# Low-rank factors as stacked f16 parts, weight maxima spread differently over the batches, and two more PSUM banks for the queries of batch 1

## The chip, the cores and the metric

The kernel runs on one core of a Trainium2 chip. Its engines work from queues of their own and wait for each other by semaphores: TensorE (PE; matrix products into PSUM), VectorE (DVE), ScalarE (ACT), GpSimd (POOL) and SyncE (SP; it only issues transfers here). The metric is the device time of one launch in microseconds; lower is better. TensorE's clock is granted at one of two levels, 1.2 and 2.4 GHz; the profile shows it as a share of the full one.

## What is computed

Eight batches of 256 tokens and 512 channels pass two layers. The first is attention with AdaLN and a 4-bit feed-forward with low-rank additions, the second a scan (Runge-Kutta) and a mixture of experts. The change is all in the first:

```python
xn = _rms_norm(x, g_norm) * (1.0 + scale) + shift
q, k, v = heads(xn @ W_qkv)                    # 16 heads of 32
q, k = _rms_norm(q, g_q), _rms_norm(k, g_k)
o = softmax(q @ k.T * d ** -0.5) @ v
x1 = o + o @ W_out
w_up = dequant4bit(w_up_q, w_up_scale).T       # (q - 7.5) * scale, 512 x 2048
y1 = x1 @ w_up + b_up + x1 @ w_up_lora_a @ w_up_lora_b      # rank 16
x2 = relu(y1)
w_down = dequant4bit(w_down_q, w_down_scale).T # 2048 x 512
y2 = x2 @ w_down + b_down + x2 @ w_down_lora_a @ w_down_lora_b
x = x + y2
...
x = x + moe(scan(cond, cond, x), Wr, Wg, Wu, Wd, Sg, Su, Sd, Wsg)
```

## The kernel before

Channels lie on the 128 partitions, tokens along the free dimension. Layer 0 (`layer0`) handles one batch after the other; each engine has its program written out by hand, and the order in it is the order of work. A batch has a part of projections and norms (chunks c = 0 to 3 of 4 heads: q and k into one PSUM bank, their squares summed per head by `head_norm`, the root by ScalarE, the product by VectorE) and a part of heads (16, in 4 groups: scores of a group, row maxima, exponentials, transposition on TensorE, copy back, weighted sums). From batch 2 on the feed-forward of the batch two before is cut in parts and put between these. Batch 0 and batch 1 have no feed-forward beside them.

**Preparing the feed-forward's weights, in batch 0.** The low-rank products are folded into the weights: W = codes x scale + A·B. There are 16 pieces of 1024 columns (8 of the up, 8 of the down weights); four are prepared in the projections of batch 0, the others with its heads 0 to 11. A piece h passes: SP loads codes and scales into one of three staging buffers (it waits until `split` of piece h - 3 is done); VectorE `unpack` (line 735); TensorE `lora` (line 521) makes two products of 512 columns in banks D[0] and D[1], f32, 16 rows deep, once `stage` says that the correction of h - 1 has read the banks; VectorE `correct` (line 743) adds them; ScalarE `weights_high` (line 383) rounds to f16; GpSimd (line 290) subtracts for the low part. VectorE's order in a head is correct(h + 4), unpack(h + 5), copy of the transposed head, and the row maximum of the group's fourth head stands behind the first copy. The factors are scaled once, by VectorE (lines 728, 729).

**Weight maxima.** The second layer's weights (33 tiles of 3 parts, 256 KB each) are read twice. First only their largest value is taken: `part_max` (line 748) is one VectorE reduction of 128x512 per part, with four loads in flight; SP loads the next when a maximum is done. `max_parts(b, at)` gives each of batches 1, 2 and 3 a third of them, 33: four after each chunk of the projections (16), and 17 spread over the 16 heads. The second reading, from batch 4 on, splits them in f16 parts.

**Banks.** Eight PSUM banks: X[0:4], Ob[0:2], D[0:2]. Queries and keys of chunk c go to Gb[c % 2] = X[c % 2], so the projection of chunk c >= 2 waits for `d_qk` of chunk c - 2. D holds low-rank products in batch 0 and feed-forward sums from batch 2 on.

## Time and profile before

| | us |
|---|---|
| median of 3 runs | 2924.39 (2912.39 to 2925.42) |
| profiled execution | 2920.94 |
| its span, first to last instruction | 2919.2 |
| PE busy | 2779.1 (95%) |
| DVE busy | 1766.6 (61%) |
| ACT busy | 1125.0 (39%) |
| POOL busy | 1334.0 (46%) |

The span is from the first to the last instruction on any engine; the execution's time has 1.7 us more around it. "PE" is the products, "PEld" the loading of the stationary operand, which overlaps them; "SPq" is SP's issuing of transfers, "x16" a number of instructions in a row that the view merges. In a timeline row the brackets tell how long the engine was idle before, and what it waited for. Names left of the arrow are written, names right of it read; `l0bank` are the eight PSUM banks, `carry` the workspace, `w_emb` also holds the normed queries and keys, `hid` and `parts_mem` are staging, `late` is where the factors lie. Batch 0's projections begin at 25.7 us, its heads at 63; batch 1 at 168, its heads at 202; batch 2 at 256.

### The profile page before, as it was taken

How to read it: one execution, taken by the hardware profiler on the slowest of the kernel's cores; microseconds unless marked ns; L12 is line 12 of the kernel's file. 1: busy time of each engine (PE TensorE's matmuls, PEld its weight loads, DVE VectorE, ACT ScalarE, POOL GpSimd, SP SyncE). 2: the span in 40 equal slices, each digit the busy share in tenths (PEclk: the TensorE clock that was granted, in tenths of full speed). 3: DMA queues.
4: the chain of work that ended last, by engine and by line, in shares of the span. 5: the costliest groups of instructions: out<-in, count | busy, mean ns of one | idle time of the engine just before them, and what ended most of it. 6: DMA issues, size and time to landing. Idle time of an engine off the chain costs nothing.

```text
span 2919.2 us, 131794 instructions
## 1 busy us (share of the span) xinstructions
PE 2779.1 (95%) x49488; PEld 2428.8 (83%) x49488; DVE 1766.6 (61%) x6291; ACT 1125.0 (39%) x4986; POOL 1334.0 (46%) x3467
## 2 busy tenths in 40 slices
PE   8877999998989999999999999999999999999998
PEld 5345776776777778999999999999999999999987
DVE  3645664565464556666666666666666666666654
ACT  2323344465444433334334333333433433433322
POOL 2310001111114666665666666666666666666600
PEclk8579999999999998999999999999999999999999
DMA  7422234354340003444443443443444444344376
GB/s 241 145 87 86 82 102 135 107 168 132 124 130 4 3 4 98 131 128 134 129 129 127 134 132 120 143 130 126 135 127 132 134 128 129 127 134 129 122 234 201
DMA packets 137226, 360.85 MB, mean 124 GB/s; under 512 B 15888, under 2 KB 24720, under 8 KB 136592
## 3 DMA queue, kind: packets, MB, share of 16 engines
q1 hardware_dynamic: 136336, 354.17, 38.5%
q8 instruction: 149, 2.44, 0.3%
q10 hardware_dynamic: 672, 3.67, 0.3%
q14 instruction: 69, 0.57, 0.1%
HBM read 323.31 MB, written 34.47 MB: 123 GB/s over the span
## 4 chain that ended last, share of the span: by engine, by line
PE 59%; POOL 5%; issue 3%; DVE 2%; ACT 0%; DMA 0%; POOLq 0%; DVEq 0%; SPq 0%
PE pscan L1360 12%; PE pd L1313 12%; PE pg L1265 12%; PE pscan L1356 11%; PE pu L1265 11%; POOL lin L1110 1%; POOL lin L1126 0%; POOL carry L1155 0%; POOL from_q L1122 0%; POOL lin L1120 0%; POOL lin L1132 0%; POOL from_q L1128 0%; POOL from_q L1137 0%; PE prouter L1375 0%; POOL lin L1141 0%
## 5 line engine op out<-in xcount | busy, mean ns | idle before, releaser
L1356 PEld LDWEIGHTS pscan<-th,carry 128*128 128x128 f16 x16384 | 550.9, 96 | 73.0 <-ACT th L1175 52.6
L1356 PE MATMUL pscan<-th,carry 128*128 128x8 f16 x16384 | 560.2, 166 | 20.4 <-ACT th L1175 9.7
L1360 PE MATMUL pscan<-th,carry 128*128 128x16 f16 x16384 | 558.2, 169 | 1.9 <-DVE th L1471 1.1
L1360 PEld LDWEIGHTS pscan<-th,carry 128*128 128x128 f16 x16384 | 482.2, 96 | 3.2 <-DVE th L1471 3.0
L1175 ACT ACTIVATE th<-state 128x32 f16<-128x32 f32 x768 | 176.0, 229 | 689.7 <-DVE state L1488 689.6
L1313 PE MATMUL pd<-hg,wbuf 128*128 128x256 f16 x3168 | 427.8, 274 | 2.3 <-DMA wbuf<-w_split 2.3
L1265 PE MATMUL pg<-qh,wbuf 128*128 128x256 f16 x3168 | 424.6, 273 | 0.0
L1265 PE MATMUL pu<-qh,wbuf 128*128 128x256 f16 x3168 | 423.1, 272 | 0.0
L1488 DVE TENSOR_REDUCE state<-pscan 128x32 f32<-128x96 f32 x768 | 197.5, 257 | 264.8 <-PE pscan L1360 261.2
L1265 PEld LDWEIGHTS pg<-qh,wbuf 128*128 128x128 f16 x3168 | 293.6, 97 | 34.9
L1265 PEld LDWEIGHTS pu<-qh,wbuf 128*128 128x128 f16 x3168 | 292.3, 97 | 31.9
L1313 PEld LDWEIGHTS pd<-hg,wbuf 128*128 128x128 f16 x3168 | 277.6, 98 | 31.5 <-issue 2.6
L1483 DVE SCALAR_TENSOR_TENSOR pscan<-pscan,lin 128x32 f32<-128x32 f32 x1024 | 203.9, 199 | 109.8 <-DVE pscan L1474 3.4
L1471 DVE TENSOR_TENSOR th<-pact,th 128x32 f16<-128x32 f32 x1024 | 190.7, 186 | 125.9 <-ACT pact L1176 122.8
L1143 POOL TENSOR_TENSOR from_q<-state,carry 128x32 f32<-128x32 f32 x256 | 90.9, 355 | 263.0 <-DVE state L1488 263.0
L1175 ACT ACTIVATE th<-carry 128x32 f16<-128x32 f32 x256 | 58.6, 229 | 333.2 <-DVE carry L1488 323.4
L444 ACT ACTIVATE w_emb<-l0bank,nmax 128x256 f32<-128x256 f32 x256 | 118.7, 475 | 134.5 <-DVE nmax L816 134.5
L296 POOL TENSOR_SCALAR spare<-parts_mem 128x512 f16<-128x512 f16 x33 | 50.8, 1538 | 258.8 <-DMA w_split<-spare 151.4
L1526 DVE SCALAR_TENSOR_TENSOR hp<-hb,wk,gates 128x256 f32<-128x256 f32 x264 | 158.0, 599 | 17.7 <-DVE hb L1519 7.6
L1137 POOL TENSOR_TENSOR from_q<-state,carry 128x64 f32<-128x64 f32 x256 | 86.3, 337 | 167.4 <-DVE state L1488 167.4
L1240 ACT ACTIVATE hg<-hp 128x256 f16<-128x256 f32 x264 | 109.7, 416 | 136.7 <-DVE hp L1526 136.7
L314 POOL PARTITION_ALL_REDUCE fs<-fs x8 | 3.0, 378 | 324.3 <-DVE fs L861 324.3
(232 smaller groups left out, 4937.1 us busy)
## 6 DMA issues: line engine op xcount, KB each, us to landing
wbuf<-w_split SPq DMA_DIRECT2D x264, 512.0 KB, 3.5
wbuf<-w_split SPq DMA_DIRECT2D x264, 384.0 KB, 3.1
parts_mem<-in_w_tiles SPq DMA_DIRECT2D x149, 256.0 KB, 3.1
w_split<-parts_mem SPq DMA_DIRECT2D x99, 256.0 KB, 2.8
late<-in_w_tiles SPq DMA_DIRECT2D x49, 256.0 KB, 3.1
w_split<-spare SPq DMA_DIRECT2D x33, 128.0 KB, 3.0
out<-oo SPq DMA_DIRECT2D x8, 512.0 KB, 3.6
xs<-in_x SPq DMA_DIRECT2D x1, 3584.0 KB, 14.4
```

The costliest lines, as they stand in the source:

```text
L444: ins = act.activation(pr[:, h % HPC, qc, :], X[h % HPC][:, qc * T:(qc + 1) * T], ACT.Exp, bias=nmax[:, h % HPC, qc:qc + 1], accum_out=psu ...
L1143: pl.tensor_tensor(ms4[:], state[3][:], c4[:], ALU.mult).then_inc(S["pchain"], 1)
L1175: act.activation(th[:, :, 0, :], v3(src[:]), ACT.Tanh, scale=unit).then_inc(S["th_ready"], 1)
L1240: act.activation(hg[:, slot, 0, :], hp[:], ACT.Identity, scale=2.0 ** -11).then_inc(S["hi_ready"], 1)
L1265: ins = mm(dst[:, 0:GT], wgu[:, slot, a, w, k, :], qh[:, q, k, :], start=(k == 0 and w == q), stop=(k == NC - 1 and w == 1))
L1313: ins = mm(pd[m // 2][:, (m % 2) * GT:(m % 2 + 1) * GT], wd[:, slot, w, m * P:(m + 1) * P], hg[:, slot, h, :], start=False, stop=False, sk ...
L1356: mm(pscan[:, 0, m * B:(m + 1) * B], clo[:, k, m * P:(m + 1) * P], th[:, k, 0, :], start=(m == 0 and k == 0), stop=False, skip_group_check ...
L1360: ins = mm(pscan[:, 0:2, m * B:(m + 1) * B], chi[:, k, m * P:(m + 1) * P], th[:, k], start=False, stop=(k == NC - 1), skip_group_check=True)
L1471: dve.tensor_tensor(th[:, :, 1, :], v3(t32), th[:, :, 0, :], ALU.subtract).then_inc(S["tl_ready"], 1)
L1483: chain(dve.scalar_tensor_tensor(pscan[:, 2, 0:W], cub, -RK[s - 1] / 3, A[u][:, s, :], ALU.mult, ALU.add), False)
L1488: dve.tensor_reduce(nxt[:], pscan[:, 0:3, 0:W].rearrange("p a w -> p w a"), AX.X, ALU.add).then_inc(S["q_ready"], 1)
L1526: dve.scalar_tensor_tensor(hp[:], hb[:], wk[:, 4:5], g, ALU.mult, ALU.mult).then_inc(S["hp_ready"], 1)
```

## The change

**Factors.** The host stacks each pair of factors three times over 80 rows, with rows of zeros between: rows 0 to 15, 32 to 47, 64 to 79. ScalarE makes an f16 rounding of all 80 rows of A and of B (`factors_high`), each with a scale that is a power of two; VectorE then replaces rows 64 to 79 of A and rows 32 to 47 of B by the f16 remainders (`low_of`). One f16 product 80 rows deep so sums high·high + high·low + low·high. Up factors are made before the first product, down factors inside the projections of batch 0. The stacks are loaded into a part of `w_dn` that isn't in use yet.

**Maxima.** `max_parts` gives batch 1 the first 16 (four per chunk, none in the heads), batch 2 the next 42, batch 3 the last 41.

**Banks.** In batch 1 alone, chunks 2 and 3 of q and k go to D[0] and D[1] (`gbank`).

```diff
-        lora_up, lora_dn = late[0:R, 0:N + H0], late[32:32 + R, 0:N + H0]
+        stacked = [w_dn[0:5 * R].rearrange("p a h n -> p (a h n)").bitcast(F32)[:, n * (N + H0):(n + 1) * (N + H0)] for n in range(2)]
+        factors = [late[0:5 * R, n * (N + H0) // 2:(n + 1) * (N + H0) // 2].bitcast(F16) for n in range(2)]
+        fa = [factors[0][:, 0:N], factors[1][:, 0:H0]]
+        fb = [factors[0][:, N:N + H0], factors[1][:, H0:H0 + N]]
...
+        def gbank(b, c):
+            return (Gb + D)[c] if isinstance(b, int) and b == 1 else Gb[c % 2]
...
         def max_parts(b, at):
-            return spread((b - 1) * TILES, TILES, at, 4, PARTS) if 1 <= b <= 3 else []
+            first, count = {1: (0, 16), 2: (16, 42), 3: (58, 41)}.get(b, (0, 0))
+            return spread(first, count, at, 4, PARTS) if count else []
...
-            for half, factors in enumerate((lora_up, lora_dn)):
-                sp.dma_start(factors, dram["lora"][half]).then_inc(S["lora"], 16)
+            sp.dma_start(stacked[0], dram["lora"][0]).then_inc(S["lora0"], 16)
             for h in range(PIECES):
                 u = h % 3
+                if h == 2:
+                    sp.dma_start(stacked[1], dram["lora"][1]).then_inc(S["lora1"], 16)
...
+            def factors_high(n):
+                act.wait_ge(S["lora_scale"], 1)
+                act.wait_ge(S["lora0"] if n == 0 else S["lora1"], 16)
+                cut = N if n == 0 else H0
+                act.activation(fa[n], stacked[n][:, 0:cut], ACT.Identity, scale=for_a[0:5 * R, n:n + 1])
+                act.activation(fb[n], stacked[n][:, cut:], ACT.Identity, scale=for_b[0:5 * R, n:n + 1]).then_inc(S["lora_high"], 1)
...
+                    if b == 1 and c >= 2:
+                        act.wait_ge(S["d_qk"], b * NC + c - 1)
                     act.activation(rh[:, c % 2], Rb[c % 2][:].rearrange("p (a t) -> p a t", a=2), ACT.Ln, scale=1.0 / DH, bias=eps).then_inc(S["achain"], 1)
...
+                    if not b and c == 1:
+                        factors_high(1)
...
             norm(0)
+            factors_high(0)
...
             def lora(h):
-                if h == 0:
-                    pe.wait_ge(S["lora_ok"], 1)
-                else:
+                if h % (PIECES // 2) == 0:
+                    pe.wait_ge(S["lora_ok"], h // (PIECES // 2) + 1)
+                if h:
                     pe.wait_ge(S["stage"], h)
...
-                        c, col = h // 2, N + h % 2 * PIECE + i * 512
-                        a, bb = lora_up[:, c * P:(c + 1) * P], lora_up[:, col:col + 512]
+                        c, col = h // 2, h % 2 * PIECE + i * 512
+                        a, bb = fa[0][:, c * P:(c + 1) * P], fb[0][:, col:col + 512]
...
-                    if c >= 2:
+                    if c >= 2 and gbank(b, c) is Gb[c % 2]:
                         pe.wait_ge(S["d_qk"], b * NC + c - 1)
...
+                link(dve.tensor_scalar(power, pairs[:, :, 1], 2.0 ** -60, None, ALU.max))
+                link(dve.tensor_scalar(kp2[:, 128:130], kp2[:, 128:130], 0x7F800000, None, ALU.bitwise_and))
+                link(dve.reciprocal(for_b, power))
+                link(dve.tensor_scalar(for_b, for_b, 0.25, None, ALU.mult))
+                link(dve.scalar_tensor_tensor(for_a, power, 4.0, fs[:, 15:17], ALU.mult, ALU.mult))
+                dve.sem_inc(S["lora_scale"], 1)
...
-                dve.wait_ge(S["lora"], 32)
-                dve.tensor_scalar(lora_up[:, 0:N], lora_up[:, 0:N], swu[0:R, :], None, ALU.mult)
-                dve.tensor_scalar(lora_dn[:, 0:H0], lora_dn[:, 0:H0], swd[32:32 + R, :], None, ALU.mult).then_inc(S["lora_ok"], 1)
+                low_of(0)
+
+            def low_of(n):
+                dve.wait_ge(S["lora_high"], n + 1)
+                cut = N if n == 0 else H0
+                a, bb = fa[n][4 * R:5 * R], fb[n][2 * R:3 * R]
+                dve.scalar_tensor_tensor(a, stacked[n][4 * R:5 * R, 0:cut], for_a[4 * R:5 * R, n:n + 1], a, ALU.mult, ALU.subtract)
+                dve.scalar_tensor_tensor(bb, stacked[n][2 * R:3 * R, cut:], for_b[2 * R:3 * R, n:n + 1], bb, ALU.mult, ALU.subtract).then_inc(S["lora_ok"], 1)
...
                         correct(c)
+                        if c == 2:
+                            low_of(1)
```

VectorE's queue at the opening, from the last scaling of biases to the first correction, before (L728 and L729 scale the factors, L735 unpacks, L743 corrects):

```order
L726 TENSOR_SCALAR vecs<-vecs,fs 128x16
L728 TENSOR_SCALAR late<-late,fs 16x512
L729 TENSOR_SCALAR late<-late,fs 16x2048
L735 SCALAR_TENSOR_TENSOR hid<-hid 128x1024
L743 SCALAR_TENSOR_TENSOR hid<-hid,fs,l0bank 128x512 x2
```

and in the changed kernel (L760 and L761 are the low parts, L767 unpacks, L775 corrects):

```order
L753 TENSOR_SCALAR vecs<-vecs,fs 128x16
L760 SCALAR_TENSOR_TENSOR late<-w_dn,spare,late 16x512
L761 SCALAR_TENSOR_TENSOR late<-w_dn,spare,late 16x2048
L767 SCALAR_TENSOR_TENSOR hid<-hid 128x1024
L775 SCALAR_TENSOR_TENSOR hid<-hid,fs,l0bank 128x512 x2
```

Two scalings in place became two subtractions, behind ScalarE's roundings; the down factors' pair stands behind the third correction now. The order of products on TensorE is the same.

VectorE's queue in the first group of heads of batch 1, before (L816 is a row maximum, L829 the copy, L748 a weight maximum, L819 the inverse of the sums):

```order
L816 TENSOR_REDUCE nmax<-l0bank 128x2 x3
L829 COPY carry<-l0bank 128x512
L748 TENSOR_REDUCE spare<-parts_mem 128x1
L816 TENSOR_REDUCE nmax<-l0bank 128x2
L829 COPY carry<-l0bank 128x512
L748 TENSOR_REDUCE spare<-parts_mem 128x1
L829 COPY carry<-l0bank 128x512
L748 TENSOR_REDUCE spare<-parts_mem 128x1
L819 RECIPROCAL rinv<-psum_e 128x8
L829 COPY carry<-l0bank 128x512
L748 TENSOR_REDUCE spare<-late 128x1
```

and in the changed kernel (L850, L863 and L853 for L816, L829 and L819):

```order
L850 TENSOR_REDUCE nmax<-l0bank 128x2 x3
L863 COPY carry<-l0bank 128x512
L850 TENSOR_REDUCE nmax<-l0bank 128x2
L863 COPY carry<-l0bank 128x512 x2
L853 RECIPROCAL rinv<-psum_e 128x8
L863 COPY carry<-l0bank 128x512
```

The four weight maxima of a group are gone; those of the projections stay as they were.

The same engine and group in batch 2, in the changed kernel (L780 is the weight maximum, L806 the hidden's low part):

```order
L863 COPY carry<-l0bank 128x512
L780 TENSOR_REDUCE spare<-parts_mem 128x1
L806 TENSOR_TENSOR hid<-l0bank,hid 128x2x256
L850 TENSOR_REDUCE nmax<-l0bank 128x2
L863 COPY carry<-l0bank 128x512
L780 TENSOR_REDUCE spare<-parts_mem 128x1 x2
L806 TENSOR_TENSOR hid<-l0bank,hid 128x2x256
L863 COPY carry<-l0bank 128x512
L780 TENSOR_REDUCE spare<-late 128x1
L853 RECIPROCAL rinv<-psum_e 128x8
L863 COPY carry<-l0bank 128x512
L780 TENSOR_REDUCE spare<-parts_mem 128x1 x2
```

Before, one maximum stood where there are two now.

## Rows read from the trace of the kernel before

**Rows 1.** Windows of the opening: length; busy PE, PEld, DVE, ACT, POOL; clock; DMA; GB/s.

```profile
63.00:89.00 26.00, 18.17 (x49) 7.50 (x48) 16.54 (x22) 8.86 (x22) 9.43 (x5) 0.59 0.93 288
89.00:116.00 27.00, 22.65 (x88) 11.08 (x88) 15.93 (x23) 9.74 (x24) 8.83 (x5) 0.63 0.48 147
116.00:142.00 26.00, 24.02 (x80) 10.09 (x80) 14.01 (x22) 7.72 (x22) 7.94 (x4) 0.50 0.30 92
168.00:202.00 34.00, 25.00 (x92) 16.37 (x95) 14.52 (x29) 9.77 (x15) 4.03 (x5) 0.98 0.24 78
202.00:245.00 43.00, 26.13 (x232) 16.72 (x232) 34.80 (x64) 18.19 (x70) 0.00 (x0) 0.78 0.41 120
256.00:344.00 88.00, 81.99 (x693) 64.31 (x695) 56.54 (x102) 38.31 (x109) 4.03 (x5) 1.00 0.31 93
```

**Rows 2.** Groups of instructions by line and shape, first 330 us: busy, mean ns, idle before.

```profile
L521 PE MATMUL l0bank<-late 16*128 16x512 f32 x64 | 47.8, 884 | 8.0 <-DVE parts_mem L743 4.9 <-DVE hid L743 3.1
L535 PE MATMUL l0bank<-late,w_up 128*128 128x256 f16 x192 | 23.3, 273 | 0.8 <-DVE hid L774 0.8
```

**Rows 3.** Timeline, one step of batch 0: start, length, engine, line, operation, idle before.

```profile
102.83 1.22 DVE L735 SCALAR_TENSOR_TENSOR hid<-hid 128x1024 f32<-128x1024 int32 x1
102.95 1.06 ACT L383 ACTIVATE w_dn<-hid 128x1024 f16<-128x1024 f32 x1 [1.58 <-DVE hid L743]
104.08 2.12 POOL L290 TENSOR_TENSOR w_dn<-hid,w_dn 128x1024 f16<-128x1024 f32 x1 [2.82 <-ACT w_dn L383]
109.06 3.78 PE L521 MATMUL l0bank<-late 16*128 16x512 f32 x4 [0.91 <-DVE hid L743]
112.88 1.40 DVE L743 SCALAR_TENSOR_TENSOR parts_mem<-parts_mem,fs,l0bank 128x512 f32<-128x512 f32 x2 [2.03 <-PE l0bank L521]
```

**Rows 4.** One timeline row of SP's queue; sizes and time to landing of two transfers.

```profile
106.61 2.38 SPq L226 DMA_DIRECT2D hid<-in_dn_s  x4
...
hid<-in_dn_s SPq DMA_DIRECT2D x20, 128.0 KB, 3.6
xs<-in_x SPq DMA_DIRECT2D x1, 3584.0 KB, 14.4
```

**Rows 5.** Timeline of the first group of heads of batch 0, VectorE and GpSimd.

```profile
72.26 1.22 DVE L735 SCALAR_TENSOR_TENSOR parts_mem<-parts_mem 128x1024 f32<-128x1024 int32 x1 [4.64 <-DMA parts_mem<-in_up_s]
82.44 2.12 POOL L290 TENSOR_TENSOR w_up<-hid,w_up 128x1024 f16<-128x1024 f32 x1 [2.49 <-ACT w_up L383]
82.84 2.80 DVE L735 SCALAR_TENSOR_TENSOR hid<-hid 128x1024 f32<-128x1024 int32 x1 [1.56 <-DMA hid<-in_up_s]
```

**Rows 6.** Timeline of the opening, VectorE and TensorE.

```profile
28.61 1.28 DVE L729 TENSOR_SCALAR late<-late,fs 16x2048 f32<-16x2048 f32 x1
31.54 1.98 PE L521 MATMUL l0bank<-late 16*128 16x512 f32 x4
40.31 5.41 PE L574 MATMUL l0bank<-carry,w_qkv 128*128 128x256 f32 x16 [0.38 <-DVE w_emb L808]
```

**Rows 7.** Timeline of batch 1, projections and first scores.

```profile
184.92 3.72 PE L574 MATMUL l0bank<-carry,w_qkv 128*128 128x256 f32 x16 [2.29 <-DVE w_emb L808]
201.75 2.09 PE L601 MATMUL l0bank<-w_emb 32*128 32x256 f32 x16 [4.43 <-DVE w_emb L808]
204.27 0.69 DVE L748 TENSOR_REDUCE spare<-parts_mem 128x1 f32<-128x512 f32 x1 [1.08 <-DMA parts_mem<-in_w_tiles]
```

**Rows 8.** Timeline of batch 1, the third group of heads ends.

```profile
231.26 0.68 DVE L748 TENSOR_REDUCE spare<-parts_mem 128x1 f32<-128x512 f32 x1
231.86 0.68 DVE L829 COPY carry<-l0bank 128x512 f32<-128x512 f32 x1
233.85 1.15 PE L601 MATMUL l0bank<-w_emb 32*128 32x256 f32 x16 [1.33 <-DVE carry L829]
```

**Rows 9.** Timeline of batch 2, heads, one wait of TensorE.

```profile
312.09 1.49 PE L535 MATMUL l0bank<-late,w_up 128*128 128x256 f16 x12 [0.23 <-DVE hid L774]
```

More of the change, by code:

```diff
@@ L142, in layer0 @@
         largest = spare[:, 0:3 * TILES]
+        power, for_a, for_b = spare[:, 128:130], spare[:, 130:132], spare[:, 132:134]
         bank = [ctx.enter_context(nc.psum_tensor(f"l0bank{i}", [P, 512], F32)) for i in range(8)]
@@ L155, in layer0 @@
                  "chain achain seq plseq "
-                 "mm_lora scaled stage split d_bounds g_bounds lora_ok "
+                 "mm_lora scaled stage split d_bounds g_bounds lora_scale lora_high lora_ok "
                  "part_in0 part_in1 part_in2 part_in3 part_out0 part_out1 part_out2 part_hi part_done part_third third_out widest gmax wscale state_in mx par coef setup").split()
@@ L416, in square @@
                     act.wait_ge(S["p_qk"], b * NC + c + 1)
-                    act.activation(sqh[:, c % 2], Gb[c % 2][:].rearrange("p (a t) -> p a t", a=2), ACT.Square).then_inc(S["a_sq"], 1)
+                    act.activation(sqh[:, c % 2], gbank(b, c)[:].rearrange("p (a t) -> p a t", a=2), ACT.Square).then_inc(S["a_sq"], 1)
                 def values():
@@ L1627, in arranged @@
     part = lambda a: np.moveaxis(rows(a), 0, 1)
+    gap = np.zeros((R, N + H0), np.float32)
+    stack = lambda m: np.concatenate([m, gap, m, gap, m], 0)
     up_q, dn_q = g("L0_ffn_w_up_q").T, g("L0_ffn_w_down_q").T
@@ L1632, in arranged @@
         "up_q": part(up_q), "dn_q": part(dn_q), "up_s": g("L0_ffn_w_up_scale").T, "dn_s": g("L0_ffn_w_down_scale").T,
-        "lora": np.stack([np.concatenate([g("L0_ffn_w_up_lora_a").T, g("L0_ffn_w_up_lora_b")], 1),
-                          np.concatenate([g("L0_ffn_w_down_lora_a").T, g("L0_ffn_w_down_lora_b")], 1)]),
+        "lora": np.stack([stack(np.concatenate([g("L0_ffn_w_up_lora_a").T, g("L0_ffn_w_up_lora_b")], 1)),
+                          stack(np.concatenate([g("L0_ffn_w_down_lora_a").T, g("L0_ffn_w_down_lora_b")], 1))]),
         "vecs": np.concatenate([part(g("cond_2048").T).reshape(P, NC * B), part(g("L0_cond_b_emb")), part(g("L0_cond_g_norm")),
```

11 lines of the change are left out of this document (6 added, 5 removed).

## The prediction

> **What bounds the kernel now.** I read the page first: TensorE is busy for 95% of the span, and most of the chain that ended last is TensorE in the second layer, which the change doesn't touch. Everything that it touches lies in the first 344 us, so the next view was a table of windows over that stretch [rows 1]. The reader is to see two regimes. From 256 us on (batch 2, the first with feed-forward products beside the attention) TensorE is busy 82 of 88 us at the full 2.4 GHz: that stage is bound by it. In batch 0 (here 63 to 142 us) and in the heads of batch 1 (202 to 245) it is not: it is busy 26 of 43 us in the latter, while VectorE is busy 35 of 43; in batch 0 the granted clock is 0.50 to 0.63, the lower level of 1.2 GHz for most of the time. A stage with no engine full is bound by hand-overs, so the third view was the timeline of a single step.
>
> A step of batch 0's heads [rows 3] is a ring between two engines. The two low-rank products of a piece (L521) start at 109.06 and take 3.78 us; VectorE's correction L743, which reads them, starts at 112.88 and takes 1.40; the next piece's product may start only then, since both use banks D. That makes 5.3 us a step, four steps are 21 us, and the other 5.2 us of a group of four heads are its scores and the weighted sums of the group before. Two groups (89 to 116, 116 to 142) take 27 and 26 us [rows 1]. The first group, 63 to 89, looks alike and isn't: its transfers are busy 0.93 of the time at 288 GB/s, and VectorE waits 4.64 us for the codes of a piece [rows 5], which queue behind the load of all other batches' x, 3584 KB that take 14.4 us to land [rows 4].
>
> **The low-rank product, heads of batch 0.** A piece has 2 products of 512 columns. As f32 they leave four records in the trace, 64 in all for 16 pieces, busy 47.8 us, 2.99 a piece. An f16 product of 256 columns is busy 23.3/192 = 0.121 us [rows 2], so 512 columns take 0.24; two take 0.49 us, or 0.97 at the lower clock, where this stage runs. 80 rows instead of 16 cost nothing, as I take it, since those f16 rows use 128. TensorE is rid of 32 to 40 us; that is the far end of the gain, not the gain.
>
> With the ring's step at 0.97 + 1.40 + 0.1 = 2.5 us, VectorE is next: per head a correction 1.40, an unpacking 1.22 [rows 3] and a copy 0.69, 3.1 us from start to start since neighbours overlap by nearly 0.1, and one more row maximum (0.6) per group. A group becomes 5.2 + 4 x 3.1 + 0.6 + 0.6 (hand-overs) = 18.8 us, if nothing else is late.
>
> Something is. Staging has three buffers, so the unpacking of piece h+3 needs the correction of h to have gone on through ScalarE (1.06), GpSimd (2.12), SP's issue (0.33 and 2.38 for five transfers) and the landing (3.6 from its own issue, so 0.6 before SP's end counts) [rows 3, 4]: 1.06 + 2.12 + 0.33 + 2.38 - 0.6 + 3.6 + 0.3 for three hand-overs = 9.2 us. VectorE comes to it after two steps, 6.2 to 6.7 us, within a group: a wait of about 2.8 us once per group (across a group's border the 5.2 us cover it). I add 0.5 for VectorE and GpSimd in each other's way: an unpacking that started 0.4 us into a GpSimd subtraction took 2.80 us, not 1.22, and ended 1.1 us after it [rows 5]. So a group takes 22.1 us and two groups 44.2, against 53: **8.8 us gained**. The ends: 0, if the loop of loads is longer than I think, and 15 us (two groups at 18.8).
>
> The Trainium skill has that last effect as a rule (GPSIMD Engine Reference, "Specifications": GpSimd's SBUF interfaces are shared with VectorE and contend with instructions that have two SBUF inputs). It speaks against this change, since shorter steps put more unpackings beside subtractions, and the two new low parts have two SBUF inputs too. Were every unpacking of the two groups held as that one was, 1.6 us, it would make 8 x 1.6 = 12.8 us and eat the whole gain of this term; the trace has one such case in 16.
>
> The group at 63 to 89 I take at 0 (ends -3 and +2): the order of bytes behind x stays, and its VectorE waits for them.
>
> **The opening.** SP now loads 800 KB of stacked factors ahead of piece 0 (before 2 x 160 KB) and as much again before piece 2. ScalarE makes the high parts (80x512 and 80x2048: 0.6 and, from 1.06 for 1024 columns, 2.0 us), VectorE adds five scalar steps (0.2 each) ahead and two low parts behind (0.7 and, from the 1.22 us of 1024 columns, 2.3) where it had two scalings, of which the larger took 1.28 [rows 6]. So the first product starts at about 33.7 instead of 31.54, but is 1.5 us shorter; behind it in TensorE's queue stand the second projection and all of batch 0, which come about 1 us late. The second projection's queries gate the third, which waited 0.38 us for VectorE [rows 6] and will wait more, so shorter products gain nothing there. The same work for the down factors lies behind the third correction, where VectorE waits for a head norm anyway. Later products give back 2 us before the scores at 63, and the wait for x's bytes swallows the difference: **0** (-2 to +4, the latter if TensorE's gap of 2 us leaves the next projection at the lower clock, where the same 16 records took 5.41 us and not 3.72 [rows 6, 7]).
>
> **Batch 1, projections.** Queries of chunks 2 and 3 go to D, so the two waits of 2.29 us before them go [rows 7]: 4.6 us. Late next: the norms through ScalarE and, between VectorE's multiplications, four maxima each, which are still there, and whose loads (four deep) land in about the time in which they are used. Before, the last four waited 1.08 us for theirs and held the first row maximum; they start earlier now, while the scores' 2.09 us run. **5.7 us gained** (ends 3 and 7).
>
> **Batch 1, heads.** VectorE loses 17 maxima. A maximum takes 0.68 us and puts the next copy 0.60 later [rows 8]. Four per group stood there; the one behind the fourth copy lay under the scores. Three are on the path to the fourth copy, after which TensorE had waited 1.33 us [rows 8]: at most 1.8 us a group. Without them the fourth head's exponentials and transposition come last, worth some 0.5. I take 1.3 a group, **5.1 us gained** (ends 0 and 7.2).
>
> **Batches 2 and 3.** They take 9 and 8 maxima more, 10.4 us of VectorE, which has 31 us idle in 88 [rows 1]. Cover is that idle time and the products that TensorE has between a transposition and the next scores. But the hidden's low part already holds TensorE for 0.23 us once [rows 9], and a maximum more in front of it or of a last copy shows there. **1.5 us lost** (0 to 10.4).
>
> **Sum.** -8.8 + 0 + 0 - 5.7 - 5.1 + 1.5 = -18.1 us. The profiled execution took 2920.9 us (span 2919.2), so 2902.8 us. The median of the runs shown is 2924.4, 3.5 us above it, so this is 0.7% under the median.
>
> **Rivals.**
> - *The loads set the pace.* Pieces take over 6 us each to come round, by queueing at SP, GpSimd and VectorE in each other's way; the heads of batch 0 keep their 53 us. For it: 0.93 busy transfers at 63 to 89, and the one held unpacking. Against it: the share falls to 0.48 and 0.30 afterwards [rows 1]. Time: 2902.8 + 8.8 = 2911.6. Chance 0.17.
> - *No such wait.* Groups of 18.8 us, the ring being the only bound: 2902.8 - 6.6 = 2896. Chance 0.17.
> - *The extra maxima land on the path* in batches 2 and 3, where TensorE is full: 10.4 instead of 1.5 gives 2911.7. Against it: 31 us idle. Chance 0.06.
> - *Slower: the clock.* With products a quarter as long TensorE stands idle for half of batch 0, and stays at 1.2 GHz through batch 0's projections and the output and projections of batch 1, which now run at 0.98 of full [rows 1]. From 168 to 202 TensorE is busy 25 us; at half clock these double, and with some 10 us in the opening that is 35 us: 2902.8 + 35 = 2938. It decides if the windows from 168 show 0.5. Against it: the clock is 0.50 to 0.63 from 63 to 142 already, with TensorE busy 70 to 92% of the time, and is full again right behind. Chance 0.04.
>
> The Trainium skill warns of this in TensorE: Matmul & The Clock Gate ("HAM oscillation"): bursts with waits between them each start at the lower clock. The trace agrees for batch 0, and by that rule its heads stay at 1.2 GHz, as my terms have it.
>
> **How the numbers follow.** Forecast 0.56, and the rivals 0.17, 0.17, 0.06, 0.04. The range 2889 to 2914 takes in all but the last and the tails. What a measurement of this kernel can tell from no change is about 0.5%, 14.6 us, so faster means under 2909.8: nearly all of the forecast and of the second rival, and little of the loads' case: 0.70. Within 0.5%: 0.26. Slower: 0.04.
>
> **What would show it.** Product records of L521's successor at 0.25 to 0.45 us; groups of batch 0 from scores to scores of 22 us, with VectorE waiting for transfers or GpSimd once in each; the first group still near 26; no wait before the third and fourth projection of batch 1 and its first scores 5 us sooner after its start; heads of batch 1 in 38 us; a stage from batch 2's start to batch 4's of the old length within 2 us. The prediction is wrong if the two groups keep 26 us, if clock windows differ from 168 on, or if anything behind batch 3 changes length.

## The result, and the profile after

The changed kernel took 2897.9 us (median of 8 runs, 2892.7 to 2908.6), the kernel before beside it 2923.5 us (8 runs, 2912.4 to 2928.3): a ratio of 0.992, 95% interval 0.9902 to 0.9937. The predicted time was 2902.8 us. The profiled execution took 2892.74 us, with a span of 2891.0 us, against 2920.94 and 2919.2 before.

I begin with a table of stages, since a stage is what the prediction put a price on. A length is the difference of two starts in the timeline of TensorE: "scores" is the first of L621's products of a group (L601 before), "output product" those of L672 behind a batch (L652), "values" those of L578 (L558).

| stage | before | after | predicted |
|---|---|---|---|
| batch 0: first projection to first scores | 37.5 | 36.7 | 0 |
| batch 0: first group of heads | 26.2 | 24.3 | 0 |
| second and third group | 53.1 | 42.5 | -8.8 |
| fourth group, to the output product | 16.0 | 16.0 | 0 |
| output product of batch 0 | 9.3 | 7.0 | 0 |
| batch 1: values and projections, to first scores | 33.9 | 29.0 | -5.7 with the next |
| first group of heads | 11.7 | 10.7 | |
| other heads, to the output product | 35.4 | 30.6 | -5.1 |
| output product of batch 1 | 7.0 | 8.9 | 0 |
| batches 2 and 3 | 199.2 | 199.9 | +1.5 |
| batch 4 to the end | 2464.1 | 2460.5 | 0 |

Of the 28.2 us between the two executions 0.8 lie ahead of the table, since the first projection starts at 24.96 us instead of 25.74. That start is no property of either kernel: over all thirteen profiles of this text it lies at 25.0 to 26.3 or at 28.2 to 30.0 us, and the changed kernel itself has 24.96 in this profile and 29.16 in a second one. The same stretches as in [rows 1], now with the stages' new bounds, in the table of windows, with the columns of [rows 1]:

```profile
61.70:86.00 24.30, 7.18 (x45) 3.93 (x44) 15.29 (x21) 9.53 (x22) 9.24 (x5) 0.64 1.01 325
86.00:107.70 21.70, 10.63 (x80) 6.68 (x80) 16.18 (x22) 9.08 (x23) 8.32 (x5) 0.74 0.66 195
107.70:128.50 20.80, 9.96 (x76) 5.52 (x76) 15.33 (x22) 8.16 (x22) 7.84 (x4) 0.66 0.37 109
151.45:180.45 29.00, 24.38 (x90) 16.45 (x88) 14.62 (x28) 9.77 (x15) 4.03 (x5) 1.00 0.28 90
180.45:221.71 41.26, 28.20 (x265) 17.82 (x265) 27.18 (x49) 18.41 (x71) 0.00 (x0) 0.76 0.13 40
230.60:318.60 88.00, 81.35 (x669) 63.64 (x667) 59.49 (x108) 38.41 (x109) 4.03 (x5) 1.00 0.37 114
```

TensorE is busy 10 us of a group where it was 23, and a group is only 5 to 6 us shorter. The group of lines for the product, which answers to [rows 2], shows the same from the other side: 11.5 us busy instead of 47.8, and 21.6 us of waiting ahead of it, for VectorE, instead of 8.0 us.

```profile
L541 PE MATMUL l0bank<-late 80*128 80x512 f16 x32 | 11.5, 448 | 21.6 <-DVE parts_mem L775 11.4 <-DVE hid L775 8.6 <-DVE late L761 1.7
```

The timeline of one step, beside [rows 3] and [rows 4], shows what a step is made of now (L775 corrects, L767 unpacks, L298 is GpSimd's subtraction, L231 and L234 are SP's loads of codes and scales):

```profile
95.09 1.40 DVE L775 SCALAR_TENSOR_TENSOR hid<-hid,fs,l0bank 128x512 f32<-128x512 f32 x2
...
96.17 0.33 SPq L231 DMA_DIRECT2D parts_mem<-in_dn_q  x1
96.40 1.22 DVE L767 SCALAR_TENSOR_TENSOR hid<-hid 128x1024 f32<-128x1024 int32 x1
96.52 1.06 ACT L391 ACTIVATE w_dn<-hid 128x1024 f16<-128x1024 f32 x1 [0.29 <-DVE hid L775]
...
96.54 0.60 PE L541 MATMUL l0bank<-late 80*128 80x512 f16 x2 [0.87 <-DVE hid L775]
96.54 2.38 SPq L234 DMA_DIRECT2D parts_mem<-in_dn_s  x4
...
98.14 1.40 DVE L775 SCALAR_TENSOR_TENSOR hid<-hid,fs,l0bank 128x512 f32<-128x512 f32 x2
...
99.59 1.03 PE L541 MATMUL l0bank<-late 80*128 80x512 f16 x2 [2.00 <-DVE hid L775]
...
100.70 2.12 POOL L298 TENSOR_TENSOR w_dn<-hid,w_dn 128x1024 f16<-128x1024 f32 x1 [0.93 <-ACT w_dn L391]
101.83 2.07 DVE L767 SCALAR_TENSOR_TENSOR parts_mem<-parts_mem 128x1024 f32<-128x1024 int32 x1 [2.30 <-DMA parts_mem<-in_dn_s]
```

From one correction to the next it is 3.05 us, which is VectorE's own work; then, once in the group, VectorE waits 2.30 us for the scales of the piece that is to come, and the unpacking behind that wait takes 2.07 us instead of 1.22, because it meets GpSimd's subtraction. The two products of a piece take 0.60 us here, and 1.03 us three microseconds later: these are the two levels of the clock (granted clock 1.00 at 96.6 to 97.1 us, 0.50 at 99.7 to 100.6).

The opening, beside [rows 6], and the projections of batch 1, beside [rows 7], are two more timelines:

```profile
30.86 2.34 DVE L761 SCALAR_TENSOR_TENSOR late<-w_dn,spare,late 16x2048 f16<-16x2048 f32 x1
...
33.26 0.61 PE L541 MATMUL l0bank<-late 80*128 80x512 f16 x2 [1.65 <-DVE late L761]
...
40.47 1.83 PE L594 MATMUL l0bank<-carry,w_qkv 128*128 128x256 f32 x5 [1.86 <-DVE w_emb L842]
```

```profile
166.08 3.62 PE L594 MATMUL l0bank<-carry,w_qkv 128*128 128x256 f32 x16
...
170.40 3.62 PE L594 MATMUL l0bank<-carry,w_qkv 128*128 128x256 f32 x16
...
180.45 1.48 PE L621 MATMUL l0bank<-w_emb 32*128 32x256 f32 x16 [4.62 <-DVE w_emb L842]
```

The first product starts 1.7 us later than it did (2.5 us, counted from the first projection), and the third projection now waits 1.86 us instead of 0.38. In batch 1 no projection waits any more, and the first scores still wait 4.62 us for the last normed queries.

### The profile page after: what moved, and what is told of

The parts are those of the page before. It is cut to its first block, busy times and chain, and to the rows that moved or that the text cites. A ratio compares the mean times of both kernels' runs of the same rounds, so it can differ in the third digit from the quotient of the medians.

```text
span 2891.0 us, 131739 instructions
## 1 busy us (share of the span) xinstructions
PE 2731.1 (94%) x49448; PEld 2410.8 (83%) x49456; DVE 1771.1 (61%) x6298; ACT 1130.1 (39%) x4990; POOL 1337.5 (46%) x3467
## 4 chain that ended last, share of the span: by engine, by line
PE 60%; POOL 5%; issue 3%; DVE 2%; DMA 1%; ACT 0%; POOLq 0%; DVEq 0%; SPq 0%
PE pscan L1394 12%; PE pd L1347 12%; PE pg L1299 12%; PE pscan L1390 12%; PE pu L1299 11%; DMA wbuf<-w_split 1%; POOL lin L1144 1%; POOL lin L1160 0%; POOL from_q L1156 0%; POOL carry L1189 0%; POOL lin L1154 0%; POOL lin L1166 0%; POOL from_q L1162 0%; POOL from_q L1171 0%; POOL lin L1175 0%
## 5 line engine op out<-in xcount | busy, mean ns | idle before, releaser
L1390 PE MATMUL pscan<-th,carry 128*128 128x8 f16 x16384 | 560.3, 166 | 20.9 <-ACT th L1209 10.3
L555 PE MATMUL l0bank<-late,w_up 128*128 128x256 f16 x1152 | 144.4, 278 | 3.8 <-DVE hid L806 3.7
```

What stands on the lines that cost most here:

```text
L555: ins = mm(D[j % 2][:, (part % 2) * T:(part % 2 + 1) * T], w_up[:, k, w, part * P:(part + 1) * P], x1s[slot][:, k, q, :], start=(k == 0 an ...
L1390: mm(pscan[:, 0, m * B:(m + 1) * B], clo[:, k, m * P:(m + 1) * P], th[:, k, 0, :], start=(m == 0 and k == 0), stop=False, skip_group_check ...
```

## The experiments

"Before" in the ratios is the kernel before, run beside each experiment on the same chip.

**Each part by itself.** e1_lora_only has the stacked f16 factors and nothing else of the change, e2_max_only the new split of the maxima, e3_banks_only the two banks (its other edits are the places that read these banks, and ScalarE's wait). e4_after_again is the changed kernel once more, to compare the three with.

```diff
 e2:
-            return spread((b - 1) * TILES, TILES, at, 4, PARTS) if 1 <= b <= 3 else []
+            first, count = {1: (0, 16), 2: (16, 42), 3: (58, 41)}.get(b, (0, 0))
+            return spread(first, count, at, 4, PARTS) if count else []
 e3:
+        def gbank(b, c):
+            return (Gb + D)[c] if isinstance(b, int) and b == 1 else Gb[c % 2]
...
-                    if c >= 2:
+                    if c >= 2 and gbank(b, c) is Gb[c % 2]:
                         pe.wait_ge(S["d_qk"], b * NC + c - 1)
```

> The changed kernel with only the stacked f16 low-rank products; the weight maxima and the banks of batch 1's queries are as before. Theory: the f32 products' ring with the correction held batch 0's heads, and this part alone gives the whole of that: two groups of heads from 26.5 us to 21 to 22, the first group 1 to 3 us shorter, batch 1's projections (34 us with its first scores) and heads (47 us up to the output product) as before; 11 to 15 us less than before in all, 0.995 in ratio. Rival (the parts need each other, or it is mostly the clock of the output product behind batch 0): under 8 us, with the difference at one place behind batch 0's heads.

> The kernel before with only the new spread of weight maxima (16, 42, 41 for batches 1, 2, 3). Theory: batch 1's heads lose 4 to 6 us, its projections nothing, batches 2 and 3 gain 0 to 2 us in length: 3 to 5 us less in all. Rival (TensorE is full in batches 2 and 3, so each added maximum shows there at 0.6 us): 4 to 6 us more in batches 2 and 3, nothing gained in all. Batch 0 is untouched in both.

> The kernel before with only chunks 2 and 3 of batch 1's queries and keys in banks D. Theory: the two waits of 2.29 us before the third and fourth projection go and nothing takes their place: the first scores of batch 1 come 4.6 to 5 us sooner after its start. Rival (VectorE's four maxima between two chunks come to lie on the path, since the chunks now follow at 4.3 us): only about 2.3 us. Everything else of the old length in both.

> The changed kernel once more, unedited, for comparison on the same chip. Theory: 24 to 27 us under before (ratio 0.991 to 0.992), with stage lengths as in its first profile; the output products behind batch 0 and batch 1 (7.0 and 8.9 us there, 9.3 and 7.0 in the kernel before) may swap, if it is the clock's phase and not the change. Rival (the clock follows from the change): they stay 7.0 and 8.9.

| kernel | median us | ratio, 95% | groups 2 and 3 of batch 0 | batch 1, values to scores | heads of batch 1 | batches 2, 3 |
|---|---|---|---|---|---|---|
| before | 2925.0 | 1 | 26.7 + 26.4 | 33.9 | 47.1 | 199.2 |
| e1 factors | 2911.8 | 0.9951 (0.9931 to 0.9971) | 24.9 + 20.9 | 33.9 | 46.6 | 199.4 |
| e2 maxima | 2920.9 | 0.998 (0.9961 to 1.0) | 23.9 + 24.3 | 33.9 | 40.8 | 202.4 |
| e3 banks | 2922.0 | 0.9988 (0.9974 to 1.0002) | 24.4 + 24.4 | 28.9 | 46.9 | 199.8 |
| e4 all | 2903.0 | 0.9914 (0.9891 to 0.9938) | 22.9 + 20.9 | 29.1 | 43.1 | 200.1 |

By the ratios the parts give 14.3, 5.9 and 3.5 us, 23.7 in all, and e4 has 25.1. With intervals of 4 to 7 us to either side that says no more than that nothing speaks against their adding up. The intervals of e2 and e3 reach to no change, so their stages are the better evidence: the banks alone take 5.0 us from the projections of batch 1, the maxima alone 6.3 us from its heads (1.0 of them in the first group, where the banks alone give 0.2), and the factors alone bring the third group to 20.9 us. The 1.0 us of the first group is thus the work of the maxima.

The table also shows something that one pair of profiles hides. e2 and e3 have the kernel before's factors, and yet their second and third groups take 24 us and not 26.5. The timeline of TensorE tells why. Before:

```profile
94.15 2.38 PE L521 MATMUL l0bank<-late 16*128 16x512 f32 x4
98.03 3.44 PE L521 MATMUL l0bank<-late 16*128 16x512 f32 x4 [0.91 <-DVE parts_mem L743]
105.58 1.98 PE L521 MATMUL l0bank<-late 16*128 16x512 f32 x4
```

and in e9_x_late_before (below), which has the same products and the same order in this group, with x loaded later:

```profile
91.27 1.98 PE L523 MATMUL l0bank<-late 16*128 16x512 f32 x4
94.75 3.78 PE L523 MATMUL l0bank<-late 16*128 16x512 f32 x4 [0.91 <-DVE parts_mem L745]
102.22 1.98 PE L523 MATMUL l0bank<-late 16*128 16x512 f32 x4
105.70 1.98 PE L523 MATMUL l0bank<-late 16*128 16x512 f32 x4 [0.91 <-DVE hid L745]
```

A piece's two products take 1.98 us at the higher clock (granted 1.00 over such a stretch) and 3.78 at the lower (0.50). How many of a group's products fall into which level differs from run to run. e2 and e3 have the kernel before's own code in this stretch, and are 4 to 5 us shorter over two groups. The two groups together take 53.1, 48.2, 48.8 and 48.8 us in the profiles of the four kernels with the f32 product (before, e2, e3, e9; mean 49.7), and 42.5, 45.8, 43.8 and 42.9 in four with the f16 one (after, e1, e4, e8; mean 43.7). So of the 10.6 us that the first pair of profiles shows, some 6 are the product and the rest goes with where the clock rose and fell. That share is worked out from means of four, and no run sets the clock.

**Is the product still on the path?** e5_twice makes each product twice.

```diff
-                    ins = mm(D[i][:], a, bb, start=True, stop=True)
+                    mm(D[i][:], a, bb, start=True, stop=True)
+                    ins = mm(D[i][:], a, bb, start=True, stop=True)
```

> The changed kernel with each low-rank product made twice (the second overwrites the first with the same values): 32 more f16 products of 512 columns, 7 us of TensorE at 2.4 GHz and 14 at 1.2. Theory: the product is off the path within batch 0's groups (a ring of 1.03 + 0.85 + 1.4 against VectorE's 3.05 a head), so only the first product of each group and those of the projections show: 1 to 4 us more than the changed kernel. Rival (the product still gates every correction): 8 to 14 us more.

Measured: 2906.5 us, ratio 0.9936 (0.9911 to 0.9961). The lines of the product show the work doubled:

```profile
L542 PE MATMUL l0bank<-late 80*128 80x512 f16 x32 | 14.6, 456 | 0.0
L541 PE MATMUL l0bank<-late 80*128 80x512 f16 x32 | 14.3, 447 | 18.5 <-DVE parts_mem L776 9.7 <-DVE hid L776 6.9 <-DVE late L762 1.9
```

The second and third group take 22.3 and 21.0 us, in the range of the changed kernel (21.8 and 20.7; 22.9 and 20.9 in e4). The wait for VectorE before the product shrank by 3 us, and the groups kept their length: inside a group the product is off the path. The median is 3.5 us above e4's, with overlapping intervals of the ratios, so the whole tells nothing more. Only the projections of batch 0 may show it, with 37.6 us where the changed kernel has 36.7; but they take 35.0 in e4, so this too is within what differs from run to run.

**What holds a group: the loop of loads.** Two experiments. e6_loads3 loads the down scales of a piece with two transfers instead of four, so that SP is done earlier:

```diff
-                    for a in range(2):
-                        for half in range(2):
-                            sp.dma_start(scales[u][half * 64:half * 64 + 64, a * N:(a + 1) * N],
-                                         dram["dn_s"][2 * (hc + a) + half].partition_broadcast(64)).then_inc(codes_in[u], 16)
+                    for half in range(2):
+                        sp.dma_start(scales[u][half * 64:half * 64 + 64, :].rearrange("p (a n) -> p a n", a=2),
+                                     pairs_s[:, hc // 2, half].partition_broadcast(64)).then_inc(codes_in[u], 16)
```

> The changed kernel with the scales of a down piece loaded by 2 transfers instead of 4, so SP issues a piece in about 1.5 us and not 2.75. Theory: the loop of loads (9.2 us) holds the third unpacking of the second and third group, which waited 2.30 and 2.02 us; each of these waits shrinks by 1.2 us or so: 2 to 3 us less. Rival (VectorE and GpSimd exclude each other): the unpacking is ready earlier, but meets GpSimd's subtraction and ends 1.09 us after it as before, or holds it up: under 0.5 us gained, unpackings of 2 us and more, or subtractions of 3.

Measured: 2904.7 us, ratio 0.9928 (0.9907 to 0.9949); groups of 22.2 and 20.9 us. The 2 to 3 us that I expected are not there. SP is done 1.1 us sooner, and the data come no sooner. The transfers' rows (size each, median us from issue to landing) of the changed kernel and then of e6:

```profile
parts_mem<-in_dn_s SPq DMA_DIRECT2D x12, 128.0 KB, 3.8
```

```profile
parts_mem<-in_dn_s SPq DMA_DIRECT2D x6, 256.0 KB, 5.2
```

and the timeline of e6, one loop:

```profile
105.68 0.33 SPq L232 DMA_DIRECT2D parts_mem<-in_dn_q  x1
106.05 1.25 SPq L234 DMA_DIRECT2D parts_mem<-in_dn_s  x2
...
110.21 2.12 POOL L298 TENSOR_TENSOR w_dn<-hid,w_dn 128x1024 f16<-128x1024 f32 x1 [0.92 <-ACT w_dn L391]
...
112.00 1.41 DVE L767 SCALAR_TENSOR_TENSOR parts_mem<-parts_mem 128x1024 f32<-128x1024 int32 x1 [2.96 <-DMA parts_mem<-in_dn_s]
```

From the codes' issue to the unpacking it is 6.3 us here and was 5.7 us (96.17 to 101.83) with four transfers. The rows say where the time went: a transfer of 256 KB lands 5.2 us after its issue, one of 128 KB 3.8. What the loop saved in issuing it lost in landing, and the experiment can't price the two apart.

But the group would not have become shorter if the data had come somewhat sooner. Compare the unpacking's end with GpSimd's in the two timelines: 103.90 us behind a subtraction that ends at 102.82, and 113.41 behind one that ends at 112.33. In both it is 1.08 us. VectorE waited 2.30 us in one and 2.96 in the other, the unpacking took 2.07 and 1.41, and the sum of wait and unpacking is 4.37 us in both. It is 4.37 or 4.38 us for this unpacking in the second and the third group alike, in e4, e5, e7, e8 and e11 too, with waits from 2.02 to 2.96 us. So the late load has a price in two parts. It makes the unpacking miss its place ahead of GpSimd's subtraction (in the changed kernel by 1.1 and 0.9 us), and then the subtraction, not the landing, sets when it ends. Within that stretch an earlier or later landing changes nothing, and the third group is 20.6 to 21.0 us in all seven profiles. This is what the rival in the expectation said. No run loads the same data just early enough, so it is read from the traces and not tried. The second group differs more (21.8 to 22.9 us), since there the fourth unpacking waits for its own data in some profiles, 0.90 us in e4.

That leaves open what the group is without any load. e10_no_reload takes it away: pieces 3 to 15 are not loaded, their unpackings read what lies in the staging buffers, and wait for GpSimd's subtraction alone.

```diff
+                if h >= 3:
+                    pass
-                if h < PIECES // 2:
+                elif h < PIECES // 2:
...
-                dve.wait_ge(codes_in[u], 16 * sum(dmas[u:h + 1:3]))
-                dve.scalar_tensor_tensor(scales[u], codes[u], 7.5, scales[u], ALU.subtract, ALU.mult).then_inc(S["scaled"], 1)
+                if h < 3:
+                    dve.wait_ge(codes_in[u], 16 * sum(dmas[u:h + 1:3]))
+                else:
+                    dve.wait_ge(S["split"], h - 2)
+                dve.scalar_tensor_tensor(scales[u], codes[u], 7.5, scales[u] if h < 3 else codes[u].bitcast(F32), ALU.subtract, ALU.mult).then_inc(S["scaled"], 1)
```

> The changed kernel without the loads of codes and scales of pieces 3 to 15 (unpackings of these pieces read the codes of pieces 0 to 2 instead, and what they add to the low-rank product is not the reference's); an unpacking waits for GpSimd's subtraction of the piece three before. Theory: the loop of loads is what holds VectorE once in each group of batch 0, by 2.0 to 2.5 us; without SP's 2.7 us and the landing of 3.6 the unpacking never waits, and the second and third full group fall from 21.8 and 20.7 to 18.3 to 19.3 us; the first, freed of x too, falls to 19 to 20. Together 9 to 11 us: 2887, ratio about 0.988. Rival: VectorE and GpSimd in each other's way set the pace, GpSimd's 2.12 us for each piece among them; the groups keep 20 us and more, only the first falls.

Measured: 2883.1 us, ratio 0.9859 (0.983 to 0.9887). The windows of its first three groups:

```profile
63.20:79.40 16.20, 7.17 (x41) 3.91 (x40) 14.94 (x22) 9.26 (x22) 9.00 (x5) 0.71 0.26 102
79.40:98.10 18.70, 10.50 (x80) 6.47 (x81) 15.36 (x22) 9.33 (x24) 8.54 (x5) 0.77 0.00 1
98.10:116.00 17.90, 11.32 (x76) 6.29 (x76) 14.39 (x22) 8.18 (x22) 7.89 (x4) 0.60 0.00 1
```

and VectorE's timeline in the second:

```profile
84.91 1.40 DVE L780 SCALAR_TENSOR_TENSOR parts_mem<-parts_mem,fs,l0bank 128x512 f32<-128x512 f32 x2
86.22 1.22 DVE L772 SCALAR_TENSOR_TENSOR hid<-hid 128x1024 f32<-128x1024 int32 x1
...
88.56 1.40 DVE L780 SCALAR_TENSOR_TENSOR hid<-hid,fs,l0bank 128x512 f32<-128x512 f32 x2
89.87 1.22 DVE L772 SCALAR_TENSOR_TENSOR hid<-hid 128x1024 f32<-128x1024 int32 x1
...
91.61 1.40 DVE L780 SCALAR_TENSOR_TENSOR hid<-hid,fs,l0bank 128x512 f32<-128x512 f32 x2
92.92 1.41 DVE L772 SCALAR_TENSOR_TENSOR parts_mem<-parts_mem 128x1024 f32<-128x1024 int32 x1
```

Inside the group VectorE runs from head to head without a wait: the third unpacking begins ahead of the subtraction and takes 1.41 us, where wait and unpacking were 4.37. The groups lose 8.1, 3.1 and 2.9 us, the first one most. This shows that the late load is what lengthens the second and third group, by some 3 us each. The rival, by which GpSimd's pace alone holds them, falls, since GpSimd does as much here; but the amount, 4.37 less 1.41 us, is set by the subtraction that the late unpacking meets.

**The first group: x.** In e1 and e4, whose order of loads is the changed kernel's, VectorE waits 6.4 and 6.1 us in the first group, for codes and scales that queue behind x. e7_x_late loads x of batch 1 alone there, and the rest behind the last piece.

```diff
-                    sp.dma_start(xv[:, :, 1:, :], dram["x"][:, :, 1:, :]).then_inc(S["xs_in"], 16)
+                    sp.dma_start(xv[:, :, 1, :], dram["x"][:, :, 1, :]).then_inc(S["xs_in"], 16)
+                if h == PIECES - 1:
+                    sp.dma_start(xv[:, :, 2:, :], dram["x"][:, :, 2:, :]).then_inc(S["xs_rest"], 16)
```

> The changed kernel, but of the input only batch 1's 512 KB are loaded beside piece 4; the other 3 MB follow the last piece. Theory: the first group of batch 0's heads (24.3 us in the first profile, 28.0 in the repeat) is held by the bytes of that load; VectorE's waits of 4.7 and 2.9 us for codes there go and the group takes 20 to 22 us: 3 to 7 us less in all. Rival (the codes' transfers are slow by themselves, or the loop of loads holds it): the group stays over 23.5 us.

Measured: 2893.3 us, ratio 0.9891 (0.9869 to 0.9913). The first group takes 21.1 us, against 24.3 and 28.0 in the two profiles of the changed kernel and 27.4 in e1. VectorE in that group:

```profile
72.14 1.23 DVE L769 SCALAR_TENSOR_TENSOR hid<-hid 128x1024 f32<-128x1024 int32 x1 [0.61 <-DMA hid<-in_up_s]
...
78.97 1.23 DVE L769 SCALAR_TENSOR_TENSOR hid<-hid 128x1024 f32<-128x1024 int32 x1 [3.69 <-DMA hid<-in_up_s]
```

The first wait, before the unpacking at 67.80, is gone; the loop of loads, here with up scales of twice the size, is left with 3.69 us.

I then thought that x had become a bound only through the short product, and tried the same edit on the kernel before.

> The kernel before, with x of batch 1 alone loaded ahead and that of batches 2 to 7 behind the last piece's codes, as in e7_x_late. Theory: in the kernel before the ring of product and correction (four steps of 5.3 us and 5.2 us of scores and sums) is as long as the load of x makes the first group, so that VectorE's wait of 4.64 us for codes lay beside it. The wait goes and the group keeps 26 us: ratio 0.999 to 1.001 to the kernel before. It is the short product that made the load of x a bound. Rival: x held the group before too, which falls from 26.2 to about 22, ratio 0.9985, and e7's gain has nothing to do with the change.

Measured: 2919.2 us, ratio 0.9983 (0.9966 to 1.0). My theory fell: the first group takes 21.7 us and not 26, by its window

```profile
64.80:86.50 21.70, 16.61 (x49) 7.01 (x48) 15.71 (x22) 9.24 (x22) 9.53 (x5) 0.64 0.85 247
```

So x set the first group of the kernel before too, which fits that the short product alone brought that group nothing (27.4 us in e1).

**How many maxima.** e8_max8 gives batch 1 only 8, and batches 2 and 3 46 and 45.

> The changed kernel with only 8 weight maxima in batch 1 (chunks 0 and 1), 46 and 45 in batches 2 and 3. Theory: the four maxima behind chunk 2 stand before the last queries in VectorE's queue and on the path, 2.4 us, and those behind chunk 3 with their wait for loads (0.8) hold the first row maximum, about 2 us more; batches 2 and 3 pay 1 us at most: 3 to 4.5 us less in all. Rival (VectorE runs out of cover in batches 2 and 3): these two take 3 us more or above, and nothing is left.

Measured: 2899.8 us, ratio 0.9919 (0.99 to 0.9938). The projections of batch 1, from the queries' start to the scores, take 20.1 us instead of 22.1 and the first group 8.5 instead of 10.7. But batch 2 takes 101.7 us instead of 100.6 and batch 3 102.2 instead of 99.3. The groups of lines over batch 2 show where they land. First the changed kernel, then e8 (the scores, and the row of the sums' inverses):

```profile
L621 PE MATMUL l0bank<-w_emb 32*128 32x256 f32 x64 | 4.6, 400 | 1.6 <-DVE w_emb L842 1.6
...
L640 PE MATMUL l0bank<-ident,rinv 128*32 128x128 f32 x64 | 2.6, 278 | 0.3 <-DVE carry L863 0.3
```

```profile
L621 PE MATMUL l0bank<-w_emb 32*128 32x256 f32 x64 | 4.6, 400 | 2.1 <-DVE w_emb L842 1.6 <-DVE carry L863 0.4
...
L640 PE MATMUL l0bank<-ident,rinv 128*32 128x128 f32 x64 | 2.6, 278 | 1.1 <-DVE carry L863 1.1
```

TensorE waits 1.2 us more for VectorE's copies, and the stage is 1.1 us longer. The 3 to 4.5 us that I expected are not there: batch 1 gives 4.2 us up to its second group, and batches 2 and 3 take 4.0 back. The 2.9 us of batch 3 are not surely the maxima's, though, since that batch takes 101.7 us in e2 and 101.9 in e5 with no more maxima than the changed kernel.

e11_x_late_max12 puts e7 together with 12, 46 and 41 maxima.

> e7_x_late with 12 maxima in batch 1 (four in each of chunks 0 to 2), 46 in batch 2, 41 in batch 3. From e8_max8, which took 8 away from batch 1 and gained 2.1 us before its first scores and 2.2 in its first group, but lost 1.1 us in batch 2 (46 instead of 42) and 2.6 in batch 3 (45 instead of 41): I expect 2.2 us in the first group of batch 1 and 0 to 1 before it, and 1.1 us lost in batch 2, none in batch 3. Together 1 to 2 us less than e7_x_late, 2891 to 2892, which is under what can be told. Rival: what batch 1 gives up shows one to one in batch 2, no change from e7_x_late.

Measured: 2890.4 us, ratio 0.9888 (0.9866 to 0.991); first group of batch 1 8.9 us, batch 2 101.8. It is the fastest of the kernels that do all of the work, 7.5 us under the changed kernel's median, but the intervals of the two ratios overlap by 0.0008 (e7's by 0.0011); against e7 nothing can be told. What makes both shorter stands in the profile: the first group of batch 0, 21.1 and 21.3 us.

## Why the prediction was right, point by point

- *Product.* Predicted 0.49 us a piece at the higher clock and 0.97 at the lower, 32 to 40 us off TensorE. Measured 0.60 and 1.03 us, and 36.3 us off (47.8 to 11.5). The 0.1 us more is the end of the pair; in e5 the products follow each other at 0.22 us in the higher clock, so that 80 rows deep cost no more than [rows 2] has for 128.
- *Groups 2 and 3.* The step chosen, "a group takes 22.1 us", measured 21.8 and 20.7. Its parts are there: VectorE's 3.1 us a head (3.05), one wait a group, priced 2.8 us (2.30 and 2.02), and 0.5 us a group for VectorE and GpSimd in each other's way (0.85 and 1.13). Together that is 3.3 us predicted and 3.15 measured in both groups. The rival without the wait was 18.8 us, and e10, without loads, has 18.7 and 17.9. The sum of the loop, 9.2 us, was good too: from the end of a piece's correction at 92.84 to the unpacking at 101.83 it is 9.0. What the prediction did not see is that its two terms aren't independent: what the wait gives up, the meeting with GpSimd takes, and 3.15 us is fixed by the subtraction and not by the loop. It had the right size here partly by luck; an edit priced by the loop's sum alone fails, as e6 did. What was off is the other end: 26.5 us of the kernel before held some 2 us of low clock that other runs don't have, so that the gain, some 6 us over several profiles, is under the 8.8 predicted while the pair of profiles shows 10.6.
- *First group.* 0 predicted, for x's bytes; -1.9 in the pair; 24.3 to 30.0 us in the profiles of six kernels with the new factors and x early, 26.2 to 27.7 in three with the old. e9 shows that x was the reason in the kernel before as well.
- *Opening.* First product at 33.7 predicted, 33.26 measured; the third projection waits 1.86 us. The stage became 0.7 us shorter, which is inside what differs from run to run (35.5 to 37.5 us in four profiles with the old factors, 35.0 to 37.6 in nine with the new).
- *Batch 1, projections.* The waits of 2.29 us went, twice, as predicted: 4.9 us by the stage, of 5.7. The other 1.1 us were to come from the last maxima no longer holding the first row maximum, and did not: VectorE still waits 0.80 us for their load (0.89 in e3, 1.08 before), and with the banks alone the first group stays at 11.5 us. Late next are the norms (4.62 us before the first scores) and the maxima, as e8 shows with 2.1 us.
- *Batch 1, heads.* 4.8 us in the three groups behind the first and 1.0 in the first, 5.8 in all against 5.1 predicted. So batch 1 gave 10.7 us of 10.8, with 1 us under the other term's name. The heads did not come down to the 38 us that the prediction named as a sign, since its window of 43 us ended 4 us before the stage of 47.1. A little of it depends on the clock (43.1 us in e4 for the whole, 41.3 in the first profile).
- *Batches 2 and 3.* Four kernels with 33 maxima each in them have 199.0 to 199.8 us, mean 199.4; seven with 42 and 41 (after, e2, e4, e5, e6, e7, e10) 199.9 to 202.5, mean 200.8: 1.4 us, against 1.5 predicted. The mean hides that five of the seven lost 0.7 and two 3.1 us. The products wait for the hidden's low part for 0.57 and 0.82 us in batch 2, where [rows 9] has 0.23.
- *Clock.* The prediction took all of batch 0's heads at the lower clock, by its terms and by the rule that it cited for them. The measurement differs: the granted clock of the two groups rose to 0.74 and 0.66, and five of their eight pairs of products took 0.60 us. It cost the sum nothing, because the product had left the path. The rival in which batch 1 stays at the lower clock did not come: its projections ran at 1.00. But the output product of batch 0, the same 32 records, takes 7.0 us at full clock and 9.3 at 0.74; it was 9.3 before and 7.0 after, and that of batch 1 went the other way (7.0 and 8.9). In e4, with the same code, they took 8.7 and 9.2. The prediction had no term for this, and by its own sign, that the clock from 168 us on stays as it was, it failed. The first pair owes only 0.5 us to it, because the two cancel.

```profile
158.50:167.83 9.33, 9.33 (x32) 7.83 (x33) 0.69 (x1) 0.00 (x0) 0.00 (x0) 0.74 0.00 0
```

is the window of that output product before, and after it is

```profile
144.47:151.45 6.98, 6.98 (x32) 6.16 (x33) 0.69 (x1) 0.00 (x0) 0.00 (x0) 1.00 0.01 2
```

By its terms the prediction was right: what it said of the ring's two next bounds, of the banks and of the maxima came within 1 us a term, the output products left out, except that the product's gain is 6 us by the means and not 8.8. The total is a weaker match than it looks. The forecast was a gain of 18.1 us on the profiled execution; the ratio says 23 us (18 to 29), and a gain of 18.1 (a ratio of 0.9938) is at the edge of its interval. The means of the stages give some 16 us (6 in the groups, 10.7 in batch 1, less 1.4 in batches 2 and 3, and under 1 us in the opening). So a part of the measured gain, some 7 us by these middle values, lies in no stage that the change is known to shorten, and that the forecast came within 5 us of the median is in part luck.

What stays open is this part. Of it 3.6 us stand in the first pair from batch 4 on, where no code differs and the prediction had named any change as a sign against it. Over all profiles that stretch takes 2463.1 to 2464.6 us in five kernels that lack at least one part of the change, and 2458.5 to 2466.7 in the eight others, so that no cause can be named.

## What to carry to other kernels

When two engines pass a piece back and forth, shortening one of them is worth the distance to the next ring, not the engine's saved time: here 36 us off TensorE were 6 to 10 us of time, because VectorE (3.05 us a head) and a late load stood right behind. Work out the next two rings before the edit, from the rows of one step. When one instruction waits, ask what it meets once it may start: here the load was late, but the subtraction in VectorE's way set the price, 3 us a group, and a load somewhat earlier would have changed nothing. And before you read a term of a few microseconds from one pair of profiles, look at the length of one unchanged instruction in both: where the clock moves between its levels, an unchanged stage of 25 us differs by 2 us by itself.

## What the runs showed of the hardware

- **An unpacking and a subtraction take turns.** An unpacking, whose inputs both lie in SBUF, takes 1.22 us. Started while GpSimd subtracts, it ended 1.08 to 1.09 us after GpSimd's end, wherever it began: 2.07 us (above, GpSimd 100.70 to 102.82), 2.35 us beside a subtraction from 122.63 to 124.75, and in e6, where it began right behind GpSimd:

```profile
91.48 2.12 POOL L298 TENSOR_TENSOR w_up<-hid,w_up 128x1024 f16<-128x1024 f32 x1 [4.65 <-ACT w_up L391]
91.63 3.06 DVE L767 SCALAR_TENSOR_TENSOR parts_mem<-parts_mem 128x1024 f32<-128x1024 int32 x1 [1.31 <-DMA parts_mem<-in_dn_s]
```

  An end that is fixed to GpSimd's, whatever the start, is that of an instruction held back rather than slowed. The Trainium skill (GPSIMD Engine Reference, "Specifications") names contention for VectorE's instructions with two SBUF inputs; the trace agrees, with up to 1.8 us here and 1.9 in e1 (3.15 us, begun 0.06 us behind GpSimd's start). A correction beside a subtraction, with one of its inputs in PSUM, kept its length (98.14, 1.40 us, beside GpSimd's 97.65 to 99.77).
- **It goes the other way too.** GpSimd's subtraction took 2.93 us instead of 2.12 where it began 0.27 us into an unpacking (40.33, 1.22 us; GpSimd from 40.60).
- **Fewer transfers landed later.** Scales as two transfers of 256 KB landed 5.2 us after their issue, as four of 128 KB 3.8 us (3.9 in e4). The codes in front of them, of unchanged size, landed after 4.1 us, against 3.7 and in e4 3.9, which is no clear difference.
